# A planned five-engine order: step costs with an added wait, a finer grain and other stage leads

## The reference

```python
h = relu(layernorm(x)); x = x + L0(h)   # deg * (h Wi + b) + adj (h Wj)
h = relu(layernorm(x)); x = x + L1(h)   # attention, one head: softmax(mask(leaky(s_i + t_j))) (h W)
h = relu(layernorm(x)); x = x + L2(h)   # attention, 8 heads of 32: softmax(mask(q k / sqrt(32))) v, then Wo
h = relu(layernorm(x)); x = x + L3(h)   # 4 graph attention heads of 256, elu, joined by W_out,
                                        # an output attention, elu, a two-layer FFN, a layer norm
```

## Time and profile before

| | us |
|---|---|
| median of 3 runs | 2095.14 (2087.29 to 2101.73) |
| the profiled execution, its own time | 2089.51 |
| its span, first to last instruction | 2087.9 |
| mean granted TensorE clock | 0.976 |

### The profile page before, as it was taken

How to read it: one execution, slowest core, us unless ns; L and a number is a source line. 1 busy time by engine, 2 the same in 40 slices (tenths; PEclk the granted TensorE clock), 3 DMA queues, 4 the chain that set the end, 5 groups by cost and what they waited for, 6 DMA issues and landing times. The chain is left out here.

```text
span 2087.9 us, 45990 instructions
## 1 busy us (share of the span) xinstructions
PE 1905.1 (91%) x15944; PEld 1781.3 (85%) x15944; DVE 1822.3 (87%) x6095; ACT 1448.2 (69%) x3378; POOL 609.8 (29%) x756
## 2 busy tenths in 40 slices
PE   1899999999999999999999999999999999999985
PEld 1789888988888989888898888889888899898874
DVE  6688999989999988989998898999889899998774
ACT  2467677777677777767777776777776677876664
POOL 4122332222332332233233233323223322322222
PEclk8899999999999999999999999999999999999997
DMA  5000000000000000000000000000000000000000
GB/s 153 11 17 11 22 22 11 22 11 22 22 22 11 22 17 17 21 22 19 14 22 17 17 22 22 12 21 22 15 18 21 21 12 22 17 12 16 17 16 11
DMA packets 31206, 43.85 MB, mean 21 GB/s; under 512 B 3328, under 2 KB 26880, under 8 KB 30976
## 3 DMA queue, kind: packets, MB, share of 16 engines
q1 hardware_dynamic: 30976, 40.91, 6.1%
HBM read 32.38 MB, written 8.52 MB: 20 GB/s over the span
## 5 line engine op out<-in xcount | busy, mean ns | idle before, releaser
L707 POOL TENSOR_SCALAR ea<-ea,rs 128x256 f32<-128x256 f32 x256 | 140.0, 559 | 476.8 <-DVE rs L1316 476.8
L691 POOL TENSOR_TENSOR rstd<-ve,pow_half 128x2 f32<-128x2 f32 x160 | 119.4, 746 | 488.3 <-DVE ve L1197 486.2
L1093 PE MATMUL ps<-kp,qp 32*128 32x256 f32 x1536 | 250.1, 295 | 3.8 <-DVE kp L1345 3.4
L852 ACT ACTIVATE pb<-lg,hmin 128x256 f32<-128x256 f32 x512 | 231.6, 505 | 19.0 <-DVE hmin L1366 18.4
L899 PE MATMUL ps<-wout,hid 128*128 128x256 f32 x1536 | 230.2, 290 | 4.2 <-ACT hid L866 4.2
L1093 PEld LDWEIGHTS ps<-kp,qp 32*128 32x128 f32 x1536 | 197.7, 185 | 41.5 <-issue 22.9
L1366 DVE CUSTOM_DVE_ANT_0 lg<-ps,maskp 128x256 f32<-128x256 f32 x512 | 195.0, 417 | 33.8 <-PE ps L1093 31.2
L899 PE MATMUL ps<-pT,whs 128*128 128x256 f32 x1536 | 213.4, 288 | 11.0 <-DVE pT L1325 9.7
L899 PEld LDWEIGHTS ps<-pT,whs 128*128 128x128 f32 x1536 | 191.7, 191 | 20.5 <-DVE pT L1325 16.2
L899 PEld LDWEIGHTS ps<-wout,hid 128*128 128x128 f32 x1536 | 197.1, 190 | 6.4 <-ACT hid L866 5.6
L729 POOL TENSOR_TENSOR hid<-fu,hid 128x512 fp32r<-128x512 f32 x96 | 127.0, 1322 | 255.9 <-ACT hid L866 255.9
(11 more groups left out here) (180 smaller groups left out, 4739.6 us busy)
## 6 DMA issues: line engine op xcount, KB each, us to landing
tbc<-t_dram SPq DMA_DIRECT2D x32, 512.0 KB, 3.6
xin<-x_in SPq DMA_DIRECT2D x32, 256.0 KB, 2.7
out<-xs SPq DMA_DIRECT2D x32, 256.0 KB, 2.2
t_dram<-tb SPq DMA_DIRECT2D x128, 1.0 KB
xs<-a_heads SPq DMA_DIRECT2D x4, 128.0 KB, 5.9
pT<-a_heads SPq DMA_DIRECT2D x4, 128.0 KB, 4.6
lg<-W_out SPq DMA_DIRECT2D x2, 256.0 KB, 5.6
tb<-adj SPq DMA_DIRECT2D x1, 256.0 KB, 2.7
```

The costliest lines, as they stand in the source:

```text
L707: last = pool.tensor_scalar(ea(g)[:, c, :], ea(g)[:, c, :], rs[g][:, c:c + 1], 1.0, ALU.mult, ALU.mult)
L852: last = act.activation(pb[h % 2][:, c, :], lg[h % 2][:, c, :], ACT.Exp, bias=hmin[h % 2][:, c:c + 1], scale=-1.0)
L1093: last = pe.matmul(bank(BA)[:, c, :], qp[r, a, oc, blk(c)], kp[r, b, oc, :], start=(n == 0), stop=(n == 2))
```

## The change

Three things in the planner; no step, wait, buffer or instruction is added or taken away.

```diff
 def a(name, k, engine, cost, *after):
-    names[name, k] = dict(..., cost=cost, ...)
+    names[name, k] = dict(..., cost=cost + ISSUE[engine], ...)
...
-GRAIN, LEAD = 0.1, (30.0, 10.0, 5.0, 10.0)
+GRAIN, LEAD = 0.02, (42.0, 28.0, -2.0, 23.0)
+ISSUE = (0.07, 0.04, 0.05, 0.05, 0.05)
```

More of the change, by code:

```diff
@@ L522, in a @@
                 def a(name, k, engine, cost, *after):
-                    names[name, k] = dict(step=(name, k, u), engine=engine, cost=cost, rest=0.0, ready=0.0, then=[],
+                    names[name, k] = dict(step=(name, k, u), engine=engine, cost=cost + ISSUE[engine], rest=0.0, ready=0.0, then=[],
                                           after=[p for p in after if p] + [(name, k - 1), ago(name, k)])
```

## The result

The changed kernel takes 1987.93 us (median of 4 runs, 1986.96 to 1992.14) against 2094.63 us before: a ratio of 0.9502, 95% interval 0.9479 to 0.9526. The forecast was 2064 with a range down to 2035. The sign was right, the size was not: 107 us were gained, not 30.

What follows compares the result with a forecast made beforehand. PE, with DVE close behind, was taken to bound the kernel, leaving 3.1 us idle a batch to win. From 2089.5 us, 30 won in the loop and 4 lost in the tail gave 2064 us, range 2035 to 2120.

Steps and rivals of the forecast that it cites:

- What bounds the kernel: Loop: PE first, DVE nearly full; an order can only win idle time, 3.1 us of each 61.4 us batch on PE.
- ISSUE: Planner's step costs raised per engine, bringing planned load near the measured one: value 0, bound 45 us either side.
- GRAIN: Planner's tie width for start times, 0.1 to 0.02 us: value 0, since PE's waits are 0.7 and 1.2 us.
- LEAD: Planner priorities: earlier layers and FFN gain 19 to 25 us of lead against layer 3, winning 30 us in the loop.
- the phase: Loop: layer 2 of batch u+2 was to start some 20 us before layer 3's output attention of batch u.
- the wait of `q`: PE idle before layer 2's product `q`, 38.9 us in all, was to fall to under 15 us.
- What is late next: Layer 3 loop: 47.1 us alone, so 14.3 us of slack in 61.4; the forecast needs it to stay inside.
- Starvation: Rival: layer 3, last choice on PE and DVE, outgrows its slack and sets the period; 2137 us, chance 0.19.
- The tail: End of the run: layer 3 of batch 30 is alone for 20 us more; 4 us lost, bounds 0 to 17.
- The head: Up to 120 us only layers 0 to 2 can run, whatever the leads: 0, with 5 us either way.
- Much more is won: Rival: with true costs PE's other waits shrink too, two thirds of 92.7 us; 2032 us, chance 0.08.
- The sum: Whole kernel: 2089.5 less 30 in the loop plus 4 in the tail, giving 2063.5, say 2064 us; chance 0.42.

Runs made afterwards that it cites:

- the fourth pair: Added engine costs (ISSUE) put into the kernel before with grain already 0.02 and old leads: 2089.5 us without them, 2160.8 us with them.
- layers01_back: Changed kernel with the lead of layers 0 and 1 put back against layer 3 (22 in place of 42): 2261.8 us, ratio 1.0818.
- port_low: Changed kernel's planner, also making clashing DVE and GpSimd steps wait for each other, with leads giving nearly the old phase: 1981.5 us, ratio 0.9446.
- lead_only: Kernel before with only the new leads, old grain 0.1 and no added ISSUE costs: 2117.2 us, ratio 1.0108.

## Why the prediction was wrong, point by point

- *What bounds the kernel.* Right that PE is first and DVE close behind; wrong that an order can only win idle time, and that the 3.1 us a batch of PE idle time are all there is to win. DVE's 55.4 us a batch were taken as fixed work. They held about 3 us of waiting for GpSimd, which the profile counts as busy. This is the step that failed in the reading. PE's busy time fell too, by 32.4 us over the span. The mean clock can't have done that: it was 0.976 before and 0.974 after. What did was not followed up.
- *ISSUE: value 0, 45 us either way.* This is the term that failed most: 44 us alone, at the edge of its bound, 128 us with the new leads (2115.8 to 1987.9), and 71 us lost in the fourth pair. The forecast had the right observation, that the old plan took PE for 8% less loaded than it is, and gave it no price.
- *GRAIN: value 0.* Measured 1 to 5 us won in three pairs, and 111 us lost with ISSUE and the old leads. The argument by size (no wait of 0.1 us seen) was void: a tie decided otherwise starts a different order, and the price of that order is not bounded by the 0.1 us.
- *LEAD: 30 us won, by the phase.* The phase moved further than forecast (31 us, forecast 15 to 25), the wait of `q` went (forecast under 15 us, measured 0.2), and `spread` to `final` fell from a median of 49.2 us to 36.5, nearer 30 than 47 as forecast. The period was not the forecast 60.4 but 57.2 us. As a cause it is refuted from three sides: leads alone moved the phase and lost 23 us; `layers01_back` had the phase and took 2261.8; `port_low` has the old phase and takes 1981.5. What goes with the new phase is that GpSimd's and DVE's clashing steps meet less (11 to 65 us of excess in the seven orders that have it, 95 to 121 in the five of the same planner that don't); the forecast gained by it without naming it, which is luck.
- *What is late next: the layer 3 loop has slack.* Right; it didn't bind. Starvation did not come.
- *The tail: 4 us lost.* 2.4 us lost, the clock much as before. Right.
- *The head: 0, 5 either way.* The first `spread` comes 18.5 us later, since steps of later batches pass layer 3 of the first one, which the bound overlooked. But PE does 16.5 us more work by then, and its idle time up to there is 61.3 us against 59.3; up to 120 us the head was as forecast (56.41 us busy in both). Counted as time lost, the head is within its bound.
- *The rivals.* "Much more is won" had the direction, with 8%, and fell 44 us short of it. Its sentence from the Trainium skill (Perfetto Trace Analysis), that weight-load time and not matmul time shows PE's distance from its limit, pointed the right way: 201 us were free by that count, and 103.6 still are (1716.8 - 1613.2).
- *The sum.* Of 107 us, the runs give 39 to fewer hold-ups (43.3 less 4.6) and 65 to the queues' order with its effect on the clock; some 3 are the difference between the chips' runs of before. The two were tried apart only in this sequence, with hold-ups removed first. Of the 65, the clock is some 10 at most by the estimate above; which waits and which denser stretches of matmuls make up the rest stays open.

## What to carry to other kernels

A list scheduler that writes fixed queues is only as good as its costs: if it thinks that engines are less loaded than they are, changing its priorities is a lottery, and once the costs include each step's overhead its own length can choose the priorities. Don't price such a change by summing its parts; one cheap tie can turn the whole order. And compare an engine's busy time for the same instructions, and each form's mean with its median: a gap can be contention, and a scheduler can keep the two parties apart.

## What was not expected of the hardware

- A DVE instruction of the kind of `normal` or `rows` that starts while a GpSimd `tensor_tensor` runs does not end before it: all 41 such `normal` ended 0.08 to 0.09 us after it, and two `rows` took 1.93 us in place of 0.73 beside one of 1.28 us. In all these are 97 us in the kernel before, and cutting GpSimd's steps to a sliver took 43 us off the whole kernel.
- Short pauses cost clock in a loop that is nearly full. In `lead_only` PE was busy 2.92 of 4 us, and the clock was 0.67 there and 0.91 in the next 4 us, in which PE was busy throughout; PE's busy time was 29.5 us longer over the span than in the kernel before, with 5 us less idle time. The slowest orders have the lowest mean clock (0.944 and 0.917). The Trainium skill (TensorE: Matmul & The Clock Gate, Part 1) has it that the clock is held up by activity alone; by that, an order with pauses pays for them again in the work behind them. The windows agree.
